# Two pairs of first-layer weights loaded in 32-wide blocks and turned by VectorE, their loads reordered over two queues, and five waits and steps moved

## What is computed

```python
xn = _layernorm(x)
s = _L0_attn_ref(xn, W_in, W_out, A_theta, B_real, B_imag, C_real, C_imag, norm_w)
g = _silu(_L0_ffn_ref(xn, W1, W2, W3))
x = x + s * g
xn = _layernorm(x)
s = _L1_attn_ref(xn, qkv, o_proj, gamma, beta)      # causal attention over 512 rows
g = _silu(_L1_ffn_ref(xn, W1, W2, W3))
x = x + s * g
```

## Time and profile before

| | |
|---|---|
| Median of 3 runs | 362.24 us (362.18 to 363.77) |
| Profiled execution, its own time | 364.02 us |
| Its span, from first to last instruction | 362.2 us |
| TensorE busy | 353.7 us, 98% |
| VectorE busy | 251.1 us, 69% |
| ScalarE busy | 167.7 us, 46% |
| GpSimd busy | 104.2 us, 29% |
| Share of the chain that ended last | TensorE 76%, VectorE 12%, ScalarE 4%, DMA 3% |
| DMA packets | 69648, of which 40692 are under 512 bytes; 34.44 MB |

### The profile page before, as it was taken

One profiled execution on the slowest core, in us unless ns is written; L12 is line 12 of the kernel. 1 busy time (PEld: TensorE's weight loads), 2 busy tenths in 40 slices (PEclk: granted clock), 3 DMA queues, 4 the chain that ended last, 5 costly groups with the idle time before them and its releaser, 6 DMA issues.

```text
span 362.2 us, 4969 instructions
## 1 busy us (share of the span) xinstructions
PE 353.7 (98%) x1785; PEld 299.6 (83%) x1785; DVE 251.1 (69%) x482; ACT 167.7 (46%) x326; POOL 104.2 (29%) x122
## 2 busy tenths in 40 slices
PE   8998899999999999999999999999999999999996
PEld 5886788888888888887888888888888888888896
DVE  5669954896479945977568894688636887356645
ACT  2865361357135624345285544644446454454510
POOL 2165310165315953474007030060300603004000
PEclk9999899999999999999999999999999999999999
DMA  7999686305252303040142501424105342054001
GB/s 238 251 183 225 154 111 57 116 2 139 36 138 39 116 2 116 3 133 14 60 144 64 144 0 58 139 67 149 57 22 168 74 123 81 0 186 112 22 3 58
DMA packets 69648, 34.44 MB, mean 95 GB/s; under 512 B 40692, under 2 KB 69624, under 8 KB 69624
## 3 DMA queue, kind: packets, MB, share of 16 engines
q1 hardware_dynamic: 69480, 34.06, 37.0%
q10 hardware_dynamic: 144, 0.07, 0.1%
HBM read 21.99 MB, written 12.12 MB: 94 GB/s over the span
## 4 chain that ended last, share of the span: by engine, by line
PE 76%; DVE 12%; ACT 4%; DMA 3%; issue 2%; SPq 1%; POOL 1%; ACTq 0%; DVEq 0%
PE GU L357 14%; PE GU L359 14%; PE GU L358 14%; PE O L357 8%; PE O L358 7%; PE O L359 7%; DVE hid L841 3%; DVE hf L997 2%; DVE rows L1015 2%; PE O L425 1%; DMA stage<-in_L_ffn_W 1%; DVE rows L914 1%; DMA swap_rows<-GX 1%; PE T L357 1%; PE T L359 1%
## 5 line engine op out<-in xcount | busy, mean ns | idle before, releaser
L721 ACT ACTIVATE hf<-GU 128x512 f32<-128x512 f32 x64 | 38.2, 598 | 80.9 <-DVE hid L841 62.7
L997 DVE TENSOR_TENSOR hf<-hf,GU 128x512 f32<-128x512 f32 x64 | 43.5, 680 | 30.9 <-PE GU L359 25.0
L841 DVE TENSOR_TENSOR hid<-hf,hid 128x512 fp32r<-128x512 f32 x64 | 52.4, 820 | 0.3
L357 PE MATMUL GU<-XT,W1T 128*128 128x512 f32 x128 | 50.5, 395 | 0.0
L359 PE MATMUL GU<-XT,W1T 128*128 128x512 f32 x128 | 49.9, 390 | 0.0
L358 PE MATMUL GU<-XT,W1T 128*128 128x512 f32 x128 | 49.8, 389 | 0.0
L357 PE MATMUL GU<-XT,W3T 128*128 128x512 f32 x128 | 49.8, 389 | 0.0
L359 PE MATMUL GU<-XT,W3T 128*128 128x512 f32 x128 | 49.8, 389 | 0.0
L358 PE MATMUL GU<-XT,W3T 128*128 128x512 f32 x128 | 49.8, 389 | 0.0
L357 PE MATMUL O<-hid,W2hi 128*128 128x512 f32 x112 | 44.1, 394 | 0.7 <-ACT U L670 0.7
L358 PE MATMUL O<-hid,W2hi 128*128 128x512 f32 x112 | 43.7, 390 | 0.0
(11 more groups left out here) (204 smaller groups left out, 724.4 us busy)
## 6 DMA issues: line engine op xcount, KB each, us to landing
swap_rows<-GX SPq DMA_DIRECT2D x7, 512.0 KB, 3.4
sT<-swap_rows SPq DMA_DIRECT2D x28, 128.0 KB, 2.7
swap_gate<-GX SPq DMA_DIRECT2D x7, 512.0 KB, 2.9
sT<-swap_gate SPq DMA_DIRECT2D x28, 128.0 KB, 2.8
stage<-in_L_ffn_W SPq DMA_DIRECT2D x12, 256.0 KB, 4.5
swap_p<-PX SPq DMA_DIRECT2D x4, 640.0 KB, 3.2
PL<-swap_p SPq DMA_DIRECT2D x16, 160.0 KB, 3.2
stage<-in_L_ffn_W SPq DMA_DIRECT2D x32, 64.0 KB, 2.7
```

The source lines that it names most:

```text
L357: pe.matmul(o, lhs(0), rhs(0), start=start, stop=False)
L721: act.activation(hf[:, c % 2, :], GU[:, c % 2, 0, :], ACT.Silu).then_inc(silu_done, 1)
L841: dve.tensor_tensor(dst, src, hi_part.bitcast(F32), ALU.subtract).then_inc(done, 1)
L997: dve.tensor_tensor(hf[:, c % 2, :], hf[:, c % 2, :], GU[:, c % 2, 1, :], ALU.mult).then_inc(mul_done, 1)
```

## The change

- W1 and W3 of the third and fourth pair (i = 2 and 3) of the first layer come through `load_blocks`, VectorE turns them in place (`first_turn`), ScalarE copies the high part from stage (`first_turned_hi`), and GpSimd subtracts the low part (`first_pair_lo`). TensorE's transposes of them fall away; those of W2 stay.
- SP's loads are in another order, and the five loads of the states, win, norm_w, gamma and beta are issued by ScalarE. They have a semaphore of their own for k_vector, kv_loaded.
- On VectorE k_vector and the turn of woutT stand further ahead, on ScalarE the scaling of win.
- GpSimd waits for the normalised rows of group 1 before the last pair's butterfly.
- `next_hadamard` writes to the T banks, and two waits of it on the drained O bank and one at the down projection are gone.
- `turn_c2` of the first attention group stands a chunk earlier.

```diff
@@ sync @@
             load_pair(0, 1, stage[:, 1, :, :], stage_loaded[1])
+            load_first_blocks(2, 0)
+            sp.wait_ge(w2_tr, 1)
+            load_first_w2(2)
+            load_first_blocks(2, 1)
             sp.dma_start(X[:, TILES:2 * TILES, :], xt_dram[:, TILES:2 * TILES, :]).then_inc(xnext_loaded, 16)
-            sp.wait_ge(w2_tr, 1)
-            load_pair(0, 2, stage[:, 0, :, :], stage_loaded[0])
-            for i, m in enumerate((A_theta, B_real, B_imag, C_real, C_imag)):
-                sp.dma_start(ssm[:, i, :, :], m.rearrange("c (a p) s -> p (c a) s", p=P)).then_inc(small_loaded, 16)
-            sp.dma_start(win[:, :, :], W_in.rearrange("(a p) k -> p a k", p=P)).then_inc(small_loaded, 16)
+            sp.wait_ge(w2_tr, 2)
+            load_first_w2(3)
+            load_first_blocks(3, 0)
+            load_first_blocks(3, 1)
             load_blocks(woutT[:, :, :].rearrange("p m d -> p (m d)"), W_out, wout_loaded)
-            sp.wait_ge(w2_tr, 2)
-            load_pair(0, 3, stage[:, 1, :, :], stage_loaded[1])
-            sp.dma_start(normB[:, :], norm_w.rearrange("(a d) -> a d", a=1).broadcast_to([P, D])).then_inc(small_loaded, 16)
...
-            sp.wait_ge(w2_tr, PAIRS - 1)
+            sp.wait_ge(hx_lo, 2)
             load_w(PAIRS)
@@ tensor @@
             def next_hadamard(i):
-                pe.wait_ge(u_ready, i)
+                pe.wait_ge(u_ready, i - 1)
                 pe.wait_ge(natx_ready, i - PAIRS + 1)
-                pe.matmul(O[:, 1, :], hadmR[:, :], ...
+                pe.matmul(T[:, i % 2, :], hadmR[:, :], ...
...
-                if first and c % 2 == 0:
-                    pe.wait_ge(w_lo, c + 2)
+                if first and c == 2:
+                    pe.wait_ge(w_lo, 4)
+                if first and c in (4, 6):
+                    pe.wait_ge(hx_lo, c - 2)
...
                 head_hadamard(1)
-                head_pair(2)
                 head_pair_w2(2)
...
                 head_hadamard(2)
-                head_pair(3)
                 head_pair_w2(3)
...
-                pe.wait_ge(u_ready, PAIRS + (0, 1, 3)[n - 1])
+                if n == 1:
+                    pe.wait_ge(u_ready, PAIRS)
...
-                        pe.wait_ge(gateT_ready, 2 * n)
                         next_hadamard(PAIRS + 2 * n - 3)
@@ scalar @@
+            def first_turned_hi(i):
+                for w, WT in enumerate((W1T[0], W3T[0])):
+                    hi(WT[:, 0, :, 2 * P * i:2 * P * (i + 1)], stage[:, i % 2, w, :].rearrange("p (k h) -> p k h", k=KC),
+                       hx_turned, 2 * (i - 2) + w + 1, hx_hi)
...
                 chunk(0, 1, True)
+                first_turned_hi(2)
                 pair_u(0, 1, 1)
-                pair_hi(0, 2, 2)
                 nat_hi(2, w2nat)
+                for i, m in enumerate((A_theta, B_real, B_imag, C_real, C_imag)):
+                    act.dma_start(ssm[:, i, :, :], ...).then_inc(kv_loaded, 16)
+                act.dma_start(win[:, :, :], ...).then_inc(kv_loaded, 16)
                 chunk(0, 2, True)
                 chunk(0, 3, True)
+                first_turned_hi(3)
                 pair_u(0, 2, 2)
-                pair_hi(0, 3, 3)
                 nat_hi(3, w2nat)
+                act.wait_ge(kvec_ready, 1)
+                for m in range(MC):
+                    act.activation(win[:, m, :], win[:, m, :], ACT.Identity, scale=kvec[:, m:m + 1]).then_inc(win_scaled, 1)
+                act.dma_start(normB[:, :], ...)      # and gamma, beta, all three to small_loaded
                 chunk(0, 4, True)
@@ vector @@
+            def first_turn(i):
+                for w in (0, 1):
+                    dve.wait_ge(stage_loaded[i % 2][w], landed(i))
+                    in_place(stage[:, i % 2, w, :]).then_inc(hx_turned, 1)
...
-                    if n >= NB - 1:
+                    if n >= NB:
                         turn_c2(n + 1)
...
+                if c == 3 and n == NB - 1:
+                    turn_c2(n + 1)
@@ gpsimd @@
+            def first_pair_lo(i):
+                for w, WT in enumerate((W1T[0], W3T[0])):
+                    pool.wait_ge(hx_hi, 2 * (i - 2) + w + 1)
+                    pool.tensor_tensor(WT[:, 1, :, 2 * P * i:2 * P * (i + 1)], stage[:, i % 2, w, :].rearrange("p (k h) -> p k h", k=KC),
+                                       WT[:, 0, :, 2 * P * i:2 * P * (i + 1)].bitcast(F32), ALU.subtract).then_inc(hx_lo, 1)
...
                 rstd_of(1)
+                pool.wait_ge(xn_ready, 3)
                 pair_butterfly(0, 3, 4)
```

More of the change, by code:

```diff
@@ L349, in _ @@
             sp.wait_ge(out_stored, 16 * (NB - 1 + len(LAST_PARTS)))
-        N_SMALL = 9
+        N_KV, N_SMALL = 6, 3
         @block.tensor
@@ L397, in next_hadamard @@
             def next_hadamard(i):
[L399 removed]
+                pe.wait_ge(u_ready, i - 1)
                 pe.wait_ge(natx_ready, i - PAIRS + 1)
[L401 to L402 removed]
+                pe.matmul(T[:, i % 2, :], hadmR[:, :], w2nat[:, 0, :, :].rearrange("p a d -> p (a d)"), start=True, stop=False)
+                pe.matmul(T[:, i % 2, :], hadmR[:, :], w2nat[:, 1, :, :].rearrange("p a d -> p (a d)"), start=False, stop=True).then_inc(h_done, 1)
             def head_hadamard(i):
@@ L744, in block0_head @@
                 chunk(0, 1, True)
+                first_turned_hi(2)
                 pair_u(0, 1, 1)
-                pair_hi(0, 2, 2)
                 nat_hi(2, w2nat)
+                for i, m in enumerate((A_theta, B_real, B_imag, C_real, C_imag)):
+                    act.dma_start(ssm[:, i, :, :], m.rearrange("c (a p) s -> p (c a) s", p=P)).then_inc(kv_loaded, 16)
+                act.dma_start(win[:, :, :], W_in.rearrange("(a p) k -> p a k", p=P)).then_inc(kv_loaded, 16)
                 chunk(0, 2, True)
                 chunk(0, 3, True)
+                first_turned_hi(3)
                 pair_u(0, 2, 2)
-                pair_hi(0, 3, 3)
                 nat_hi(3, w2nat)
+                act.wait_ge(kvec_ready, 1)
+                for m in range(MC):
+                    act.activation(win[:, m, :], win[:, m, :], ACT.Identity, scale=kvec[:, m:m + 1]).then_inc(win_scaled, 1)
+                act.dma_start(normB[:, :], norm_w.rearrange("(a d) -> a d", a=1).broadcast_to([P, D])).then_inc(small_loaded, 16)
+                act.dma_start(gbrow[0:KC, :], gamma.rearrange("(a p) -> a p", p=P)).then_inc(small_loaded, 16)
+                act.dma_start(gbrow[KC:2 * KC, :], beta.rearrange("(a p) -> a p", p=P)).then_inc(small_loaded, 16)
                 chunk(0, 4, True)
@@ L756, in block0_head @@
                 hi(gb[:, :, :].rearrange("p g k -> p (g k)"), O[:, 0, 0:2 * KC], gb_tr, 1, gb_ready)
-                act.wait_ge(kvec_ready, 1)
-                for m in range(MC):
-                    act.activation(win[:, m, :], win[:, m, :], ACT.Identity, scale=kvec[:, m:m + 1]).then_inc(win_scaled, 1)
                 chunk(0, 6, True)
@@ L1081, in block0_head @@
                 nat_lo(1, w2nat)
+                first_turn(2)
                 chunk(0, 1)
-                pair_lo(0, 2, 2)
                 nat_lo(2, w2nat)
                 chunk(0, 2)
+                first_turn(3)
                 chunk(0, 3)
+                k_vector()
+                nat_lo(3, w2nat)
                 dve.wait_ge(xnext_loaded, 16)
-                pair_lo(0, 3, 3)
-                nat_lo(3, w2nat)
                 stats(1, TILES)
@@ L1092, in block0_head @@
                 normalise(1, TILES)
-                k_vector()
+                turn_wout()
                 chunk(0, 5)
-                turn_wout()
                 x_turn(1)
```

27 lines of the change are left out of this document (17 added, 10 removed).

## The result

The changed kernel takes 363.82 us in the median of 15 runs (363.3 to 365.99), the kernel before on the same chip 362.18 us (15 runs, 361.92 to 364.0). The ratio is 1.0042, with a 95% interval from 1.0023 to 1.006: slower by 0.4%, inside the 0.5% that a measurement of this kernel can't well tell from no change. The profiled execution took 363.32 us, 0.7 less than that of before (364.02).

A forecast was written before the change was run, and what follows sets the result against it. TensorE, busy 98% of the span, was taken as the bound, VectorE close behind in the head. 362.24 + (48.7 - 46.85) - 1.1 = 363.0, shaded to 362.7 us; range 359.2 to 365.2.

The forecast's parts named there:

- late kvec: Head, VectorE: k_vector's result at about 30.6 us, its products and hid(2) taking turns with GpSimd's subtractions and butterflies.
- the two gaps: Head, TensorE: waits for nat_lo(3) until 31.3 and gamma and beta until 33.6, some 3.9 us instead of 2.4.
- The base: Median run of the kernel before, 362.24 us, taken as lacking the 1.59 us half-clock cost; its mix starts at 46.85.
- Loads: Head: pair 2's W3 lands at 15.0, pair 3's at 22 to 22.5 (wanted 24.2); no cost.
- The step that failed: Head, TensorE: chunk 6 ends at 36.65, product of win and woutT (L425) at 37.15; savings of 1.74 and 2.4 eaten up.
- one rival's worst: Rival that the lock costs more (chance 0.24): mix at 50.1, 364.4 us; half clock adds up to 1.6, giving 366.0.
- After that VectorE is the later one: Head behind L425: VectorE's chain sets the end, last product ready at 48.1, or up to 2.0 later, 50.1.
- hid(4) won its race: Head: hid(4) at 37.7 against the wide butterfly at 37.65; winning gives 48.1, losing makes each step up to 2.0 later.
- my 48.7: Likeliest start of the mix at the head's end, middle of the lower half of 48.1 to 50.1; likeliest case's chance 0.43.
- The later waits: Behind the head: waits at the down projection (0.7) and ZT (0.4) go, -1.1 us in all.
- The rule of the Trainium skill: VectorE-GpSimd lock without turns: kvec at 29.2, sum 1.4 lower at 361.6; chance 0.1.
- the second queue: Loads over two queues: by the skill only issue time is saved, no transfer; here it moves onto ScalarE, in the chain.

The follow-up runs named there:

- e2: The kernel before with only the edits behind the head (T banks, dropped waits, turn_c2 a chunk earlier): 361.17 us, ratio 0.9953.
- e3: The changed kernel with the four subtractions of pairs 2 and 3 on VectorE instead of GpSimd: 362.56 us, ratio 0.9996.
- e12: The changed kernel with idle products in TensorE's two long gaps (5 and 12), every wait kept: 361.94 us, ratio 0.9966.
- e9: e4 with six idle products ahead of chunk 6 and the five ssm loads issued at the program's start: 361.58 us, ratio 0.9975.
- e5: e4 with VectorE's product 4 and nat_lo(3) ahead of k_vector, ScalarE reordered, GpSimd's wait for normalised rows dropped: 365.36 us, ratio 1.0081.
- e10: e5 with GpSimd's wait for the normalised rows put back: 362.41 us, ratio 0.9995.
- e4: The changed kernel with small loads issued early by SP and the four subtractions on VectorE: 360.84 us, ratio 0.9945.

## Why the prediction was right, and where it wasn't

I said 362.7 us (sum 363.0; 363.2 for the profiled execution) and no difference to be told. It is 363.82 and 363.32. The waits and, in the main, their causes were right: late kvec, the two gaps before the Hadamard product and before gamma and beta, none left behind the head. What happens behind the gaps was not: I left the slow clock out, and so had the wrong engine set the end of the head. With the later waits sized too small the errors have opposite signs, and that the time comes out so near is in part luck.

- **The base.** I read the two values of the earlier trace rows and the three runs as one kernel with and without a slow stretch. The two groups of before's 35 runs, with their clocks, fit it (e2), though only a run with the slow stretch has a trace. I put its price at 1.59; the sixteen passes take 3.27 us at full clock (40.07 to 43.34), not 3.44, which makes it 1.76, and the groups lie 2.1 apart.
- **Loads.** Pair 2's W3 landed at 15.08 (I said 15.0). Pair 3's landed at 24.46 instead of 22 to 22.5, after the 24.2 at which it was wanted: the earlier trace rows has landings of 2.4 to 3.1, but all eight quarters of pair 3 took 3.9 to 4.6. It cost only the 1.55 us turn, 0.26 more than 1.29. win landed at 27.80, not by 26, a wait of 0.45, and so its load begins the chain that set the head.
- **kvec** at 30.5, as I said (30.6), by turns with GpSimd: products of 0.77 and hid(2) of 1.68 us. That two causes make it up, win's landing and the turns, is shown by e3: without the turns it was ready at 29.27, with win waited for until 28.09.
- **The two gaps.** 4.3 us where I had 3.9. gamma and beta landed for 34.84 instead of 33.6, since the landing took 3.3 and not 2.6.
- **The step that failed** is "ending at 36.65, and then L425 at 37.15 instead of 37.23": I let chunk 6 run at full clock behind 3.9 us of gaps, with the 1.59 for 2.4 us of gap just priced, and kept the slow clock for one rival's worst. Chunk 6 took 5.03 us instead of 2.8, and the product came at 40.07. e12 takes the slow clock away: chunk 6 in 2.90 us, and 1.9 less in all. All runs of the changed kernel show a mean clock of 0.985 to 0.991.
- **"After that VectorE is the later one"** fails with it. TensorE waits for nothing from 34.84 to the mix at 49.53, so its own passes set the mix and not VectorE's chain. hid(4) won its race as I took for likeliest, by 0.05 us (37.53 against 37.58), so little that it is luck; hid(5) lost against the widest butterfly and took 2.62. Neither moved the mix: qkv was turned by 45.37, 0.9 us before TensorE took it at 46.26. That 49.53 lies only 0.8 from my 48.7 is luck; with chunk 6 as in e12 it would be 47.4, an estimate from 35.04 and e12's 12.35 us from there to the mix.
- **The later waits** were all gone, as said, but worth 1.6 to 2.0 us (e2) and not 1.1. I priced the stalls by their shown idle time; the earlier trace rows gives 0.35 for one that cost 0.60. c2's transfer was issued 2.6 us earlier than before (151.5 against 154.1), for the 1.9 that I had.
- Against the profiled time this makes 364.02 + 1.09 - 2.0 = 363.1, measured 363.32. Against the median it makes 362.18 + (49.53 - 46.85) - 2.0 = 362.9, measured 363.82: the profiled execution is the second lowest of the changed kernel's fifteen runs. What makes the others up to 2.7 us longer, at mean clocks of 0.985 to 0.991, no trace shows.
- **The rule of the Trainium skill** on the lock (SBUF — State Buffer, "SBUF: two separate sides") was put at 0.1: k_vector's three products took 0.78, 0.77 and 0.77 us, each behind one GpSimd instruction, so turns it is, as in the earlier trace rows. On the second queue, the Trainium skill (DMA: Bandwidth & Descriptors, "Issuing engines are not separate DMA queues") agrees with the trace as far as it shows it: the issue time only moved to ScalarE, which stands idle for 2.61 us before silu 2.

Not tried was the changed kernel without GpSimd's new wait; U was ready at 35.92 there and the butterfly began at 36.07, so it could hardly cost there. Why pair 3's quarters landed so late stays open, but ScalarE's ssm loads aren't the reason: the first quarter, issued at 14.72 and 3.3 us before the first of them, took 4.2 us already, and in e9, without them in that stretch, the eight took 3.6 to 4.8.

## What to carry to other kernels

- Where a gap of TensorE is foreseen that is as long as these, price the clock behind it as a term of its own, for all work that follows at once, and ask anew which engine then sets the end; filling the gap with idle products takes the slow clock away (1.9 us in e12) when the gap itself can't be.
- A load behind a wait in an engine's queue leaves only when that wait is over. Put loads that wait for nothing ahead of it, even on the busiest queue: three lines were worth 2.7 us.
- Price a stall of TensorE from start to start of the passes around it, not by the idle time that the profile shows. Look for what VectorE and GpSimd do at the same time before moving work to the one that seems free.

## What was not expected of the hardware

- VectorE's normalise operations with one SBUF tensor in (128x256, 0.41 us) wait for GpSimd as those with two do: four took 5.92 us beside the butterflies and 1.37 us without (e5, e10).
- The kernel before shows the lower mean clock (0.994 to 0.995) in 11 of 35 runs and not in the others, though its source is the same; its one trace, of a run with it, has a gap of 2.40 us, and how long the gap is in the others isn't known. With the gaps of 1.4 and 2.9 us the lower clock comes in all 15.
- ScalarE's issues of loads, 0.53 us each in the changed kernel, took up to 1.76 us in e5, where product 2 was late by 1.7 us against e4; a queue in the path of a silu brings its jitter with it.
